# Steps 8 to 46 of an attention pipeline: shorter and fewer unread products, and a second halved maximum behind each halved one

## The reference, cut to what matters

```python
x = _layernorm(x + mixer(x))                  # state-space mixer: chunks, decays, gate, rms norm, W_out
x = _layernorm(x + cross_attention(x, ctx))   # 16 heads of 8: softmax(q k^T / sqrt(8)) v, W_o
x = _layernorm(x + experts(x))                # gate, top 2 of 8 experts, silu(x w0) * (x w1), wo
```

## Time and profile before

| | us |
|---|---|
| median of 3 runs | 413.25 (412.43 to 416.03) |
| the profiled execution's own time | 414.47 |
| its span | 413.1 |
| PE busy | 348.0 (84%), 3092 records |
| DVE busy | 274.1 (66%), 809 records |
| ACT busy | 228.4 (55%) |
| POOL busy | 184.0 (45%) |
| mean granted clock of PE | 0.968 of 2.4 GHz |

### The profile page before, as it was taken

One profiled execution on the slowest core, in us unless ns is written; L12 is line 12 of the kernel. 1 busy time (PEld: TensorE's weight loads), 2 busy tenths in 40 slices (PEclk: granted clock), 3 DMA queues, 4 the chain that ended last, 5 costly groups with the idle time before them and its releaser, 6 DMA issues.

```text
span 413.1 us, 9146 instructions
## 1 busy us (share of the span) xinstructions
PE 348.0 (84%) x3092; PEld 251.6 (61%) x3092; DVE 274.1 (66%) x809; ACT 228.4 (55%) x397; POOL 184.0 (45%) x281
## 2 busy tenths in 40 slices
PE   1998899999999999888878898997698899999900
PEld 1556676666545455444444455686598799999900
DVE  3446666888888898788778635455458455665527
ACT  2586666342675665464546485643445576676304
POOL 2763588744545452544260504153534433233325
PEclk9999999999999999999999999998979999999975
DMA  8700657623514040505474421011111221110054
GB/s 265 267 0 17 204 165 234 198 80 120 165 61 137 5 142 3 161 11 164 142 249 136 150 50 33 14 47 34 40 33 47 84 80 48 53 53 27 27 175 144
DMA packets 43694, 41.99 MB, mean 102 GB/s; under 512 B 3792, under 2 KB 37648, under 8 KB 43648
## 3 DMA queue, kind: packets, MB, share of 16 engines
q1 hardware_dynamic: 40368, 35.09, 27.6%
q0 software_dynamic: 2272, 4.69, 3.2%
q10 hardware_dynamic: 1008, 1.61, 1.1%
HBM read 26.36 MB, written 14.75 MB: 100 GB/s over the span
## 4 chain that ended last, share of the span: by engine, by line
PE 55%; DVE 20%; issue 9%; ACT 6%; another core or an unknown queue 5%; POOL 3%; DMA 2%; SPq 0%; ACTq 0%; DVEq 0%; POOLq 0%
PE banks L1057 15%; PE banks L1082 8%; DVE nm L1251 6%; PE banks L898 4%; PE banks L731 4%; PE banks L958 4%; PE banks L794 3%; PE banks L845 2%; PE banks L988 1%; PE banks L889 1%; PE banks L866 1%; ACT probs_all L1551 1%; DMA vals<-y_dram 1%; PE banks L1046 1%
## 5 line engine op out<-in xcount | busy, mean ns | idle before, releaser
L1551 ACT ACTIVATE probs_all<-banks 128x1024 f32<-128x1024 f32 x64 | 65.4, 1022 | 43.7 <-PE banks L898 34.8
L1057 PE MATMUL banks<-xT,w_tile 128*128 128x128 f32 x624 | 79.5, 281 | 1.0 <-issue 1.0
L1251 DVE TENSOR_REDUCE nm<-banks 128x4 f32<-128x1024 f32 x56 | 68.3, 1219 | 17.2 <-PE banks L889 10.9
L1057 PEld LDWEIGHTS banks<-xT,w_tile 128*128 128x128 f32 x624 | 74.7, 195 | 2.4 <-issue 2.3
L1726 POOL DMA_INDIRECT y_dram<-x,scatter_u x39 | 37.8, 969 | 67.8 <-DVE x L1395 65.9
L1377 DVE SCALAR_TENSOR_TENSOR ctx_in<-ctx_in,banks 128x512 f32<-128x512 f32 x39 | 26.8, 687 | 38.7 <-ACT ctx_in L1595 32.3
L1082 PE MATMUL banks<-w_down,hidT 128*128 x312 | 43.5, 284 | 1.1 <-DVE hidT L1384 1.1
L1595 ACT ACTIVATE ctx_in<-banks 128x512 f32<-128x512 f32 x39 | 23.3, 597 | 38.0 <-PE banks L1057 27.4
L1588 ACT ACTIVATE w_tile<-w_up 128x1024 f32 x39 | 41.3, 1058 | 1.8 <-issue 0.3
L1721 POOL DMA_INDIRECT slots_dram<-rows,place_u x32 | 31.5, 986 | 23.0 <-DVE count L1342 15.7
L898 PE MATMUL banks<-scores_in 32*128 32x256 f32 x256 | 33.7, 326 | 9.6 <-ACT probs_all L1551 4.9
(11 more groups left out here) (223 smaller groups left out, 669.2 us busy)
## 6 DMA issues: line engine op xcount, KB each, us to landing
scores_in<-k_dram SPq DMA_DIRECT2D x8, 512.0 KB, 4.2
scores_in<-q_dram SPq DMA_DIRECT2D x8, 512.0 KB, 4.2
w_up<-in_L_ffn_w SPq DMA_DIRECT2D x16, 256.0 KB
cs_wide<-cs_dram SPq DMA_DIRECT2D x14, 256.0 KB, 3.9
xg<-slots_dram SPq DMA_DIRECT2D x39, 65.0 KB, 1.8
k_dram<-probs_all SPq DMA_DIRECT2D x8, 256.0 KB, 2.5
q_dram<-split_qk SPq DMA_DIRECT2D x8, 256.0 KB, 2.3
w_down<-in_L_ffn_wo SPq DMA_DIRECT2D x8, 256.0 KB
```

What stands on the lines that cost most here:

```text
L1057: m = TE.matmul(up_bank(i, j)[:, c * P:(c + 1) * P], w_tile[:, i % WS, j * FF + c * P:j * FF + (c + 1) * P], xT[:, i % XT, :], start=True, ...
L1251: V.tensor_reduce(most, scores_of, AX_X, ALU.max, negate=True).then_inc(s["nmax"], 1)
L1551: C.activation(probs(n).rearrange("p j k q -> p (j k q)"), EXPS, ACT.Exp, scale=SCALE).then_inc(s["probs"], 1)
```

## The change: widths, counts and one more pair of halves

`UNREAD_IN_MIX` gets shorter entries in the steps 8, 9, 16 and 24 and loses those of the steps 13, 17 and 21. The second product of `unread_step` stays in step 11 alone. DVE's reduction of each follower is cut in two like the one ahead of it; its first half waits for a new semaphore `max_bank`, which PE raises when the follower's first bank is complete, its second half for `max_mm`.

```diff
-UNREAD_IN_MIX = {1: S, 4: S, 5: P, 8: 3 * P, 9: S, 13: 3 * P, 16: 3 * P, 17: 3 * P, 21: S, 24: 3 * P}
+UNREAD_IN_MIX = {1: S, 4: S, 5: P, 8: S, 9: P, 16: S, 24: P}
...
-                for _ in range(1 + (n > 4 and n % PAIRS_B < GR)):
+                for _ in range(1 + (4 < n < PAIRS_B * 2 and n % PAIRS_B < GR)):
                     TE.matmul(AV[:, S:2 * S], ident, kv[:, 0:S], start=True, stop=True)
...
                         m = maximum(later, k, i)
+                        if by_bank and first == 0 and second == 1:
+                            m.then_inc(s["max_bank"], 1)
                         if last:
                             m.then_inc(s["max_mm"], 1)
...
-                q.wait_ge(s["max_mm"], n + 1)
+                if n - 1 in IN_HALVES:
+                    q.wait_ge(s["max_bank"], IN_HALVES.index(n - 1) + 1)
+                else:
+                    q.wait_ge(s["max_mm"], n + 1)
...
+                if n - 1 in IN_HALVES:
+                    V.tensor_reduce(most[:, 0], scores_of[:, 0], AX_X, ALU.max, negate=True)
+                    q.wait_ge(s["max_mm"], n + 1)
+                    V.tensor_reduce(most[:, 1], scores_of[:, 1], AX_X, ALU.max, negate=True).then_inc(s["nmax"], 1)
+                    return
                 V.tensor_reduce(most, scores_of, AX_X, ALU.max, negate=True).then_inc(s["nmax"], 1)
```

More of the change, by code:

```diff
@@ L357 @@
     "y_mm y_sum y_gated sq yT_t yT rms_in rms out_mm r1 ln1_var ln1_in ln1 x1 x1_t x1T "
-    "q_mm max_mm max_half nmax nm_split nm_t nm_out exp_mm probs av_mm av_lo av_hi heads_t o_norm o_t oT wo_mm "
+    "q_mm max_mm max_bank max_half nmax nm_split nm_t nm_out exp_mm probs av_mm av_lo av_hi heads_t o_norm o_t oT wo_mm "
     "r2 ln2_var ln2_in ln2 x2 x2_t x2T rows_x2 gate_mm logit ge topped chosen rank_mm counted "
```

## The result

| | before | changed |
|---|---|---|
| median of 20 runs, us | 414.7 (412.4 to 417.1) | 418.1 (413.1 to 425.9) |
| ratio, 95% interval | | 1.0057 (1.0033 to 1.0082) |
| profiled execution: its own time, span | 414.47, 413.1 | 416.06, 414.7 |
| mean granted clock in it | 0.968 | 0.956 |

The account below looks back on a forecast made before the run. The chain was read as changing hands between PE (55%) and DVE (20%), so most unread products were free. Terms -0.05 - 0.38 + 0.06 = -0.37 us gave 412.9 us, range 409.3 to 417.3, likeliest 411.5 to 414.5.

Parts of the forecast that it names:

- Prices: PE time per unread product: 0.63 us for 256 columns, 0.84 for 384, 0.43 for a pair's second; 5.08 removed in all.
- Mixer's bank worth nothing but step 8: Narrower or dropped products in 9, 13, 16, 17, 21 and 24 give 0; step 8 gives 0.05 us, bounds 0 and 0.21.
- One product in 19: Scores of step 20 are PE-bound, so one product for two in step 19 gains 0.38 us.
- in 27: One product for two in step 27: scores 0.43 us sooner, DVE late and reducing no earlier: 0, bounds 0 and 0.43.
- 35 and 43: One product for two in steps 35 and 43 lies beside a remote wait: 0, bounds 0 and 0.86 us.
- Halved followers worth nothing: Eight follower reductions on DVE in halves: seven gains end in idle time, step 27 costs +0.06 us.
- I take the clock to hold: Granted clock stays 1.00 until 277 us though PE's longest silence, ahead of step 36, grows from 1.2 to 1.6 us.
- Rival B: Clock falls to half in step 35 or 43, 4.4 us each: 417.3 for one place, 421.7 for both; chance 0.13.
- C: PE's time counts nearly everywhere, so all 5.08 us are gained: 408.2 us; chance 0.06.
- D: The followers' 0.45 us each pass on in all eight, 3.6 us gained: 409.3 us; chance 0.06.
- E: Halves begin no earlier as DVE is late everywhere, costing up to 0.48 us: 413.3; chance 0.64 together with the forecast.
- A: The remote wait ends with PE's queue, not POOL, so 35 and 43 give 0.43 us each: 412.0; chance 0.11.

Follow-up runs that it names:

- e1: The kernel before with one unread product for two in steps 35 and 43 alone: 393.5 us, ratio 0.9968.
- e3: The kernel before with the followers' reductions in halves and every unread product as before: ratio 1.0001, 0 of 12 executions fell to a mean clock under 0.965.
- e2: The changed kernel with the second products of steps 35 and 43 put back: ratio 0.9986, in two groups, 393.0 to 394.1 and 398.0 to 399.8 us.
- e12: The changed kernel run again, nothing altered: 5 of 12 executions fell to a mean clock under 0.965, one of them 403.1 us; no ratio given.
- e8: The kernel before with 256 columns in step 8 and one unread product in 19, 35 and 43: 393.2 us, ratio 0.9959.
- e11: The kernel before with 256 columns in step 8 and one product in 19, 27, 35 and 43, no halves: 6 of 12 executions fell; no ratio given.
- e15: The kernel before with the remote wait rebuilt (waiting for POOL's split), three products in 35 and 43 and one in 19: 396.9 us, ratio 1.0069.
- e6: The kernel before with one unread product for two in step 27 alone: 0 of 12 executions fell, the two longest 396.3 and 396.6 us; no ratio given.
- e10: The changed kernel with the mixer's bank list as before: 6 of 12 executions fell to a mean clock under 0.965; no ratio given.
- e14: The kernel before with the remote wait rebuilt (waiting for POOL's split) and one unread product for two in 35 and 43: 397.4 us, ratio 1.0087.
- e5: The changed kernel itself on another chip: ratio 1.0008, seven executions at 392.2 to 393.3 us and five at 397.8 to 398.4.
- e9: The changed kernel with step 24 back at 384 columns: 6 of 7 executions fell to a mean clock under 0.965; no ratio given.

## Why the prediction was wrong, by its own steps

- **Prices (0.63, 0.84, 0.43 us; 5.08 in all): right.** Where a product's time shows (idle time of step 14: 0.84 more; step 28: 0.44 sooner; steps 36 and 44 in e1: 0.43 each) it is that.
- **Mixer's bank worth nothing but step 8: right.** Steps 8 to 10 gave 0.17 in place of 0.05: the term was mis-sized, since the start of DVE's reduction can overlap the end of what stands ahead of it by 0.08 (124.96 for 124.17 + 0.87 = 125.04), which was counted in step 19 and not here: 0.16 of room for the 0.08 read.
- **One product in 19: right** (0.42 measured, 0.38 taken); **in 27: right as time** (0).
- **35 and 43: right for the set in which the result was taken** (3.92 and 3.88 us behind steps 35 and 43, 3.88 and 3.93 before), where ACT goes on 5.86 and 5.82 us behind POOL's first scatter, as predicted. Without the remote wait they are worth 0.86 together (e1), the upper bound that was given.
- **Halved followers worth nothing: right** as time, and e3 shows it for the whole. The size read for them, 0.4 to 0.5 us sooner in six steps, was right in step 7 alone (0.54); in the other five it is 0.15 to 0.17, since both banks are complete within 0.24 us there. The +0.06 in 27 is there on DVE (3.17 us from the follower's start to the next reduction, 3.11 before), but DVE came out of its remote wait 0.06 sooner after POOL's first scatter, and steps 27 to 29 take 6.88 us in both.
- **"I take the clock to hold": this step failed.** It put the clock at 0 us; in the profiled execution three falls cost 3.1. I argued from the longest silence of PE, which grows only from 1.2 to 1.6 us, and from no window below 1.00 in one execution of before. The silence was read short (PE waits 1.23 us ahead of step 44 and 1.40 in step 27, at 177.0 us, in that very trace), and the longest one is no guide: the clock holds behind those 1.40 us, and in e2 it falls behind 1.11 us ahead of the scores of step 29, in e3 behind 0.77. The second was one draw: of the executions of one program some fall and some don't, so one trace at 1.00 says nothing of how near it is. Rival B named the mechanism, gave it 0.13 and looked for it only in 35 and 43. The changed kernel's trace has it there (2.0 us) and behind step 59 (1.0 us); on the other chips it is behind step 27, costs 4.5 us there (steps 30 to 35 take 16.2 us in e12 and 11.7 in e8) and comes in 34 of 67 executions.
- **Rival B's price of 4.4 us** is near those 4.5 by luck. It was meant for 6.8 us at half speed, in which at most 3.4 us can be lost; the 4.4 hold for a fall of 11.2 us. In the two places that it named, the falls lasted 3.4 us and cost 1.2 and 0.9, where it had half of 4.4 for that length; the 4.5 belong to 13.6 us at half speed in another place.
- **The place.** The 2.4 us of the result were taken in the first set of runs, with falls behind 35, 43 and 59; the experiments, on other chips, have theirs behind 27. That the change lets the clock fall is shown for both; which removed product does it is shown for the second alone.
- **The rule of the Trainium skill** that was weighed (TensorE: Matmul & The Clock Gate, Part 1: The HAM clock gate), that activity lifts the clock from its default of half speed, is borne out by e8 against e11 (0 of 9 and 6 of 12): the product that was free as time was the one that held the clock. How soon activity lifts it is another matter: in e2 PE is busy 1.99 or 2.00 of 2 us in every window from 182 to 194 us, and the clock stays at 0.50 until 195.
- **The base** was a median of three runs, 1.45 us below that of twenty; with the 2.4 us of the ratio that makes 417.1, at the very end of the range, and the plain median (418.1) lies outside it.
- Rivals C and D fell with the timelines, E with step 7, where the halves do begin sooner, and A with the trace in which its release stays at 5.8 us with one product fewer, and with e15.

What stays open. Why 27 alone (e6) is safe and 27 with 19 is not: with one product in 19 everything behind comes 0.43 sooner, and the steps 21 to 30 have the same lengths in e6 as in e10. No run has one product in 19 and 27 with nothing else changed; e10 (with halved followers) and e11 (with step 8 shorter) have in common only these two and the ones in 35 and 43, which come behind the start of the fall. Whether the second products of 35 and 43 hold the clock across a remote wait (e14). Whether the third fall, at 256 us, belongs to the change at all: nothing was changed near it, and only the first set of runs shows one there. How often short falls come, with and without the change; the count by mean clock doesn't see them.

## What to carry to other kernels

A product that nobody reads and that lies in a wait costs nothing and may be what keeps the clock up: take out those that lie on the path (e8), and leave those that are free unless many executions show that they do nothing. Where a granted clock can fall, look at many executions and count the falls by their mean clock; one trace at full speed, or a median over two groups, hides a loss of 5 us in every second run. And halving an instruction pays only if the next thing on its engine doesn't wait for somebody else.

## What the runs showed of the hardware that was not expected

- The same program takes 394.2 to 394.8 us on three chips and 414.7 in the first set. The traces of the first set have waits of ACT and DVE that the profile calls "remote", each ending 5.8 to 5.9 us behind the first of four indirect DMAs of POOL; the others have none, though the DMAs look the same (0.95 to 1.3 us each). What it is, no run shows. And these waits are the smaller part: against e6, which takes as long as before on its chip, the trace of before is 6.5 us longer from step 3 to 63 and 13.4 us longer behind step 63 (147.3 for 133.9 us), where it has the clock at half from 280 and 298 us on and e6 has it at 1.00.
- A fall costs by its length: 4.5 us for 13.6 at half speed (e12, steps 30 to 35; the medians of the two groups of e5 lie 5.15 apart), 0.9 to 1.2 for 3.4 (the changed kernel, steps 37 to 38, 45 to 47 and 60; e3, step 34). That is 0.26 to 0.35 us lost per us at half speed, in mixer work in which PE never stops as well as in steps in which PE and ACT take turns.
- The long falls come whole or not at all: in e2, e5, e9 and e12 no execution lies between 394.1 and 396.9 us. Between the two groups there are few: 395.5 in e10, 396.3 and 396.6 in e6, all at a mean of 0.973.
